# A new order for the first slots of a cross attention, and f32 products as three bf16 products in a local attention

## The chip, the cores and the metric

The kernel runs on one core of a Trainium2 chip. The metric is the device time of one execution in microseconds, the median of several. The span of a profiled execution is a little shorter than its device time. One record of a trace says which engine did what from when to when: TensorE (PE, its weight loads PEld), VectorE (DVE), ScalarE (ACT), GpSimd (POOL) and SyncE (SP), whose queue here issues nearly all transfers.

## The reference, cut to what matters

The model has two layers on a state `x` of 4 batches x 128 tokens x 512. Layer 0: cross attention from the state (the latents) to 2048 context rows per batch, self attention, mixture of experts. Layer 1: a second cross attention, a local attention, a quantised feed-forward network. The change touches the first stage and the last but one.

```
# layer 0, cross attention (16 heads of 64); ctx: 4 x 2048 x 512
xn  = layernorm(ctx) * g_x + b_x
ln  = layernorm(layernorm(x)) * g_l + b_l         # the state is normed twice
q   = rmsnorm(ln @ Wq) ;  k, v = concat(xn @ Wkv, ln @ Wkv) ; k = rmsnorm(k)
x   = x + softmax(q k^T + mask) v @ Wout + bout
# layer 1, local attention
h   = layernorm(x)
q, k, v = h @ Wq.T + bq, h @ Wk.T + bk, h @ Wv.T + bv
ph  = running mean of h inside chunks of 32 tokens
pk, pv  = ph @ Wpk.T + bpk, ph @ Wpv.T + bpv
x   = x + attention over 16 best earlier tokens, the last one and the last phrase
```

## The kernel before

The kernel is written instruction by instruction with semaphores; each engine has its own instruction list, and the stages (`cross0_attend`, `self0`, `experts`, `cross1_attend`, `local1`, `ffn1`) follow one another with a barrier between them.

`cross0_attend` is a software pipeline over slots n. A slot of unit u (4 heads of one batch, 17 tiles of 128 rows, 16 units) is `project(n)` on TensorE: keys and values of one tile of 128 context rows (the 17th tile is the latents), in 12 products of bf16 pairs (high x high, high x low, low x high). ScalarE copies the result (`copies`), VectorE takes the low half of the values (`values_low`). Everything else is hung into the slots by tables: `ln_stat`, `ln_rstd`, `ln_norm`, `ln_turn` for the norm and transposition of one quarter (512 rows, j = 0 to 3) of a batch's context; `k_sum`, `k_norm`, `k_turn` for the norm and transposition of the keys; `k_max` for the row maxima; `q_unit`, `q_copy`, `q_norm`, `q_turn`, `q_store` for the queries, which are computed once for all batches; `w_part` for splitting the weights of four heads into high and low halves (`weights_high` on ScalarE, `weights_low` on GpSimd). Scores of tile n run 25 slots behind (`LAG`), so slots 0 to 24 have no scores; the maximum of a unit must be done (`less_maximum`) before slot 25. Slots -8 to -1 (`FIRST` on) are the head: they only bring the first context quarters and the latents.

The order inside a slot is that of each engine's list. On TensorE: `project`, `turn` of keys, `context` turns, `turn_latents`, `query_turn`, `query_product`, then values, scores, maxima. Key turns and context turns share one bank of PSUM (`KT` = 5), each waits until the one before it has been read (`before_turn`, `before_ln`). On VectorE: `values_low`, `key_low`, `maximum`, `key_norm`, `key_sum`, `context_norm`, `context_stat`, the latents' norm, the query steps. A step of SP's list waits like any other: what stands behind it is issued later.

The state is normed twice by the helper `Norm`: statistics, variance plus 1e-5, square root on ScalarE, reciprocal, scaling in place; in slots -7 and -6, that is on VectorE ahead of the scaling of context's first quarter. `turn_latents` and the latents' affine step (`latents_turned`) stand in slot -2, the first query product in slot 0.

In `local1` the state is normed (`Norm`), turned by the helper `Turn` (16 transpositions, ScalarE copies them to `HT` in f32), TensorE makes the prefix sums (`L2672`), then three projections of 4 outputs x 4 chunks in f32 (line 2685: q, k from `HT`, pk from `PT_`), scores, and two sets of values (line 2703). Four of the five weights are loaded during `cross1_attend`, the fifth at the stage's start. GpSimd has no part in it.

Of the kernel before, what the change touches and what calls it, by code (L numbers as in the profile page):

```python
# [15 lines left out]
P = 128  # L16
B = 4
# [99 lines left out]
def cross0_attend(nc, t, X, keep, sb, sem):  # L117
# [47 lines left out]
    junk = late_part(16, 1)  # L165
    Dg = late_part(17, 1).rearrange("p (h q) -> p h q", q=P)
    less = late_part(18, 1)
    ao = late_part(19, 2).bitcast(F32).rearrange("p (k n) -> p k n", n=256)

    q_sq = late_part(0, 4).bitcast(F32).rearrange("p (k n) -> p k n", n=512)  # L170
# [20 lines left out]
    ln = Norm(sb, sem, "a0ln")  # L191
# [50 lines left out]
    for u in range(UNITS):  # L242
        for j in range(5):
# [14 lines left out]
    for k in range(B * QN):  # L258
        q_unit[k].append(k)
        q_copy[k + 1].append(k)  # L260
    for b in range(B):
        q_norm[2 * b + 3].append(b)
        q_turn[2 * b + 4].append(b)
        q_store[2 * b + 5].append(b)
    for g in range(1, QUADS):
        w_part[2 * g - 2].append(g)
# [3 lines left out]
    for b in range(B):  # L270
        for j in range(4):
            at = 4 * j - 6 if b == 0 else NT0 * (4 * (b - 1) + j)
            delayed = b == 1 and j == 0
            for i in range(4):
# [3 lines left out]
                ln_turn[at + 1 + i if b == 0 else at + ((25, 26, 29, 30) if delayed else (16, 17, 21, 22))[i]]\  # L278
                    .append((b, j, i))
            ln_rstd[at if b == 0 else at + (17 if delayed else 9)].append((b, j))  # L280
            if b == 0:
                mask_block[10 + j].append((b, j))
# [52 lines left out]
    with nc.Block() as block:  # L335

        @block.sync
        def _(sp):
# [117 lines left out]
            sp.dma_start(L, t["x"].rearrange("b p d -> p b d")).then_inc(lx_in, 16)  # L456
# [3 lines left out]
            sp.dma_start(mcol8[:], t["mask0_col"]).then_inc(vec_in, 16)  # L460
# [8 lines left out]
            load(0, 2)  # L469
            weights(2)  # L470
            latents_out()
            latents(0)
            weights(3)
            load(0, 3)
            sp.wait_ge(zero_done, 2)
            for n in range(LAST):
                for b in q_store[n]:
                    queries_out(b)
                if n == 6:
                    queries(0)  # L480
                    queries(1)
                if n == 9:
# [8 lines left out]
                for b in range(1, B):  # L491
# [4 lines left out]
                    for j in range(4):  # L496
                        if n == ((7, 11, 32, 41)[j] if b == 1 else NT0 * (4 * (b - 1) + j) - 10):
# [16 lines left out]
        def _(pool):  # L514
# [39 lines left out]
            def weights_low(g):  # L554
                pool.wait_ge(w_hi_done, g + 1)
# [2494 lines left out]
```

## Time and profile before

| | |
|---|---|
| median of 3 runs | 2519.19 us (2517.22 to 2527.97) |
| the profiled execution | 2523.05 us, its span 2521.2 us |
| mean granted clock of TensorE | 0.963 |
| TensorE busy | 2302.3 us, 91% of the span |
| VectorE, ScalarE, GpSimd busy | 1821.0, 1566.5, 1129.7 us |
| first product of `project` | 37.68 us after the span's start |
| first `less_maximum` | 157.55 us |
| `local1`, from its first instruction to the last sum | 2357.3 to 2456.5 us |

The page cuts the span into 40 slices of 63 us; a digit is the busy share of a slice in tenths. Views of a stretch give the busy time of each engine in it. A timeline line has its start, its duration (of a group of instructions with "xN"), the engine, the line, what is written and read, and in brackets how long the engine had been idle and what ended that.

### The profile page before, as it was taken

Reading aid. Unit: us, or ns where it says so; the run is one execution under the profiler, and the core shown is the slowest. Engines: PE = TensorE matmul, PEld = TensorE weight load, DVE = VectorE, ACT = ScalarE, POOL = GpSimd, SP = SyncE. Lnnn points to the kernel's source line nnn. Section 1 sums busy time; section 2 is a strip of 40 time slices with the busy share of each in tenths; the row PEclk is TensorE's granted clock in tenths of the full one; section 3 lists DMA queues with packets and bytes.
Section 4 is the critical chain, followed back from the end, with each engine's and each line's share of the span. In section 5 each row is a group of like instructions: output and inputs, shape, how many; then the busy total and the mean of one; then the engine's idle time right before and its main releaser. Section 6 shows DMA issues by size and latency. Waiting matters only on the chain. (4 is left out here: it accounts for less than half of the span.)

```text
span 2521.2 us, 57561 instructions
## 1 busy us (share of the span) xinstructions
PE 2302.3 (91%) x21955; PEld 1492.9 (59%) x21955; DVE 1821.0 (72%) x3374; ACT 1566.5 (62%) x2925; POOL 1129.7 (45%) x897
## 2 busy tenths in 40 slices
PE   5899999999999999998888799994899899998795
PEld 2456656666566656665445677772567676776442
DVE  6778878887788777776363899986677777766236
ACT  4556666666666666665233599983477676787313
POOL 4546676667666664555000000004467676756100
PEclk9999999999999999999889799997999999998897
DMA  6323432233322321124330799975433444224002
GB/s 206 96 54 97 119 95 67 66 87 102 90 75 76 99 75 42 39 59 149 122 126 10 265 369 363 363 273 184 146 108 118 128 121 130 89 90 160 29 1 86
DMA packets 248819, 313.56 MB, mean 124 GB/s; under 512 B 63313, under 2 KB 174545, under 8 KB 247649
## 3 DMA queue, kind: packets, MB, share of 16 engines
q1 hardware_dynamic: 244592, 301.75, 37.0%
q10 hardware_dynamic: 3312, 6.03, 0.6%
q8 instruction: 175, 2.87, 0.5%
q0 software_dynamic: 640, 2.10, 0.3%
q14 instruction: 100, 0.81, 0.1%
HBM read 226.23 MB, written 47.91 MB: 109 GB/s over the span
## 5 line engine op out<-in xcount | busy, mean ns | idle before, releaser
L581 POOL TENSOR_TENSOR a_late<-a_late 128x512 bf16<-128x512 f32 x272 | 316.0, 1162 | 357.1 <-ACT a_late L641 356.4
L959 PE MATMUL ps<-w,a_xlo 128*128 128x512 bf16 x1088 | 412.4, 379 | 0.0
L957 PE MATMUL ps<-w,a_xhi 128*128 128x512 bf16 x1088 | 412.3, 379 | 0.0
L958 PE MATMUL ps<-w,a_xhi 128*128 128x512 bf16 x1088 | 412.3, 379 | 0.0
L2155 POOL TENSOR_TENSOR a_plo<-a_p,a_phi 128x512 bf16<-128x512 f32 x256 | 306.6, 1198 | 178.2 <-ACT a_phi L2192 169.4
L607 ACT ACTIVATE a_kraw<-ps 128x256 f32<-128x256 f32 x272 | 104.2, 383 | 367.9 <-PE ps L959 366.2
L2287 DVE CUSTOM_DVE_ANT_0 a_junk<-ps,a_biasrow 128x512 bf16<-128x512 f32 x256 | 175.9, 687 | 116.5 <-PE ps L2427 113.0
L718 DVE TENSOR_TENSOR a_v<-ps,a_v 128x256 bf16<-128x256 f32 x272 | 114.2, 420 | 160.9 <-ACT a_v L609 159.4
L2187 ACT ACTIVATE a_p<-ps,a_mcol 128x512 f32<-128x512 f32 x256 | 174.8, 683 | 86.8 <-PE ps L2445 78.9
L531 POOL TENSOR_TENSOR a_rn<-a_rn,a_power 128x16 f32<-128x16 f32 (+1 forms) x80 | 204.9, 2561 | 6.6
L732 DVE SCALAR_TENSOR_TENSOR a_kraw<-a_kraw,a_rn 128x1024 f32<-128x1024 f32 (+1 forms) x80 | 154.2, 1928 | 74.2 <-POOL a_rn L531 74.2
L637 ACT ACTIVATE a_late<-ps,a_mcol 128x512 f32<-128x512 f32 x256 | 178.8, 698 | 20.9 <-PE ps L1011 10.6
L784 DVE CAST ps<-a_late 128x512 f32<-128x512 bf16 x256 | 174.3, 682 | 12.2 <-ACT a_late L637 12.2
L959 PEld LDWEIGHTS ps<-w,a_xlo 128*128 128x128 bf16 x1088 | 106.5, 98 | 128.4
L958 PEld LDWEIGHTS ps<-w,a_xhi 128*128 128x128 bf16 x1088 | 106.4, 98 | 125.5 <-issue 2.7
L2410 PE MATMUL ps<-a_whi,c_hi 128*128 128x128 bf16 x1024 | 179.1, 220 | 1.3
L2410 PE MATMUL ps<-a_wlo,c_hi 128*128 128x128 bf16 x1024 | 178.8, 220 | 0.0
L2410 PE MATMUL ps<-a_whi,a_clo 128*128 128x128 bf16 x1024 | 178.7, 219 | 0.0
L641 ACT ACTIVATE a_late<-a_late 128x512 bf16<-128x512 f32 x272 | 171.3, 630 | 8.7
L760 DVE CUSTOM_DVE_ANT_0 a_late<-ps,a_mrow 128x512 bf16<-128x512 f32 x256 | 173.7, 679 | 0.7
L2192 ACT ACTIVATE a_phi<-a_p 128x512 bf16<-128x512 f32 x256 | 161.3, 630 | 8.1
L957 PEld LDWEIGHTS ps<-w,a_xhi 128*128 128x128 bf16 x1088 | 106.5, 98 | 99.3 <-issue 1.7
(444 smaller groups left out, 6882.7 us busy)
## 6 DMA issues: line engine op xcount, KB each, us to landing
e_wst<-in_L_ffn_W SPq DMA_DIRECT2D x46, 2048.0 KB, 10.4
a_ks<-a_khi SPq DMA_DIRECT2D x256, 64.0 KB, 2.0
a_ks<-a_klo SPq DMA_DIRECT2D x256, 64.0 KB, 2.0
a_ct<-in_ctxT SPq DMA_DIRECT2D x16, 1024.0 KB, 7.3
a_ks<-k1h_d SPq DMA_DIRECT2D x128, 128.0 KB, 2.5
xa<-in_ctx SPq DMA_DIRECT2D x8, 1024.0 KB, 5.7
a_xn<-in_ctx SPq DMA_DIRECT2D x8, 1024.0 KB, 5.5
k1h_d<-a_khi SPq DMA_DIRECT2D x64, 128.0 KB, 1.9
```

What stands on the lines that cost most here:

```text
L531: pool.tensor_tensor(rn[:, key_part(j)], rn[:, key_part(j)], power[:, key_part(j)], ALU.pow)\
L581: pool.tensor_tensor(p_lo[:, m % 3, :], p32[:, m % 2, :], p_hi[:, m % 3, :], ALU.subtract)\
L637: act.activation(p32[:, m % 2, :], ps[:, m % 2, :], ACT.Exp, **bias).then_inc(exp_done, 1)
L760: dve.tensor_tensor_reduce(junk[:], ps[:, bank_m(x), :], mrow[:, j * 512:(j + 1) * 512], 1.0, -3e38, ALU.add, ALU.max, mx[:, h, j:j + 1]). ...
L784: dve.tensor_copy(ps[:, m % 2, :], less[:]).then_inc(seeded, 1)
L957: pe.matmul(out, x_hi[:, c, tile], w_hi[:, c, g, :], start=(c == 0), stop=False)
L958: pe.matmul(out, x_hi[:, c, tile], w_lo[:, c, g, :], start=False, stop=False)
L959: last = pe.matmul(out, x_lo[:, c, tile], w_hi[:, c, g, :], start=False, stop=(c == C - 1))
L2155: pool.tensor_tensor(p_lo[:, m % 3, :], p32[:, m % 2, :], p_hi[:, m % 3, :], ALU.subtract)\
L2187: act.activation(p32[:, m % 2, :], ps[:, m % 2, :], ACT.Exp, bias=mcol[:, u // 4, s:s + 1])\
L2287: dve.tensor_tensor_reduce(junk[:], ps[:, bank_m(x), :], biasrow[:, u // 4 % 2, j * 512:(j + 1) * 512], 1.0, -3e38, ALU.add, ALU.max, mx[: ...
L2410: last = pe.matmul(ps[:, VP, i * P:(i + 1) * P], x[:, b % 2, c, tile], w[:, 1, c, quad], start=(c == 0 and k == 0), stop=(c == C - 1 and k ...
```

## The change

Two parts. In `cross0_attend`:

- The two norms of the latents become one with its own variance: norm of a norm has the variance v/(v+e), and `1.0 + 1e-5` and `1e-10` account for both (`latents_stat`, `latents_norm`). Their place is behind context's first quarter.
- The low half of the first weight is made by VectorE, behind context's first quarter; those of weights 1 to 3 are made in slots 3, 6, 9 (before 0, 2, 4) by GpSimd.
- The second quarter's turns go to slots 0, 1, 2, 2 (before -1 to 2), `turn_latents` to slot 1, all query steps two slots later, the first key turns to slots 10 to 13 (before 8 to 11), the maxima of quarters 0 to 2 two per slot from slot 14 (before those of quarters 0 and 1, from slot 12).
- In the slot, context turns that follow key turns go behind the query product, and the second context turn of a slot too.
- SP's list: first weight ahead of the state, second quarter ahead of it too, third quarter ahead of the small loads of the query norms.

In `local1`: tokens, prefix means and the five weights are each split into a high and a low half in bf16, and each f32 product becomes three bf16 products. ScalarE makes high halves, VectorE the tokens' low halves, GpSimd the rest.

```diff
-                    k_turn[e + (5 if (u, j) == (0, 0) else 3) + pr].append((u, j, pr))
+                    k_turn[e + ((7, 5, 3, 3)[j] if u == 0 else 3) + pr].append((u, j, pr))
                 for h in range(4):
-                    k_max[12 + 2 * j + h // 2 if u == 0 and j < 2 else e + 5 + h].append((u, j, h))
+                    k_max[14 + 2 * j + h // 2 if u == 0 and j < 3 else e + 5 + h].append((u, j, h))
...
-        q_unit[k].append(k)
-        q_copy[k + 1].append(k)
+        q_unit[k + 2].append(k)
+        q_copy[k + 3].append(k)
...
-        w_part[2 * g - 2].append(g)
+        w_part[3 * g].append(g)
...
-            at = 4 * j - 6 if b == 0 else NT0 * (4 * (b - 1) + j)
+            at = (-6, -3, 2, 6)[j] if b == 0 else NT0 * (4 * (b - 1) + j)
...
-                ln_turn[at + 1 + i if b == 0 else at + ((25, 26, 29, 30) if delayed else (16, 17, 21, 22))[i]]\
+                ln_turn[at + ((3, 4, 5, 5)[i] if j == 1 else 1 + i) if b == 0 else at + ((25, 26, 29, 30) if delayed else (16, 17, 21, 22))[i]]\
...
             load(0, 0)
-            sp.dma_start(L, t["x"].rearrange("b p d -> p b d")).then_inc(lx_in, 16)
             weights(0)
...
             load(0, 1)
+            sp.dma_start(L, t["x"].rearrange("b p d -> p b d")).then_inc(lx_in, 16)
...
             weights(1)
+            load(0, 2)
             for dst, src in ((gq, t["L0_xattn_qn_g"]), (gk, t["L0_xattn_kn_g"])):
...
             latents_out()
+            load(0, 3)
             latents(0)
             weights(3)
-            load(0, 3)
...
                 if n == -6:
-                    ln.vector(dve, step, L, L, 2)
+                    dve.wait_ge(w_hi_done, 1)
+                    dve.tensor_tensor(w_lo[:, :, 0, :], wst[:, 0], w_hi[:, :, 0, :], ALU.subtract).then_inc(w_lo_done, 1)
+                if n == -4:
+                    latents_stat()
                 if n == -2:
+                    latents_norm()
+                if n == 1:
                     latents_low()
...
+                ahead = 0 if k_turn[n] else 1
+                for b, j, c in ln_turn[n][:ahead]:
+                    context(b, j, c)
                 for k in q_unit[n]:
                     query_product(k)
+                for b, j, c in ln_turn[n][ahead:]:
+                    context(b, j, c)
```

and in `local1`:

```diff
+            def weights_low(k):
+                pool.wait_ge(w_hi_done, k + 1)
+                pool.tensor_tensor(w_lo[:, k], w[k], w_hi[:, k], ALU.subtract).then_inc(w_lo_done, 1)
+
+            weights_low(0)
+            weights_low(1)
+            for c in range(C):
+                pool.wait_ge(pt_hi_done, c + 1)
+                pool.tensor_tensor(pt_lo[:, c, :], PT_[:, c, :], pt_hi[:, c, :], ALU.subtract).then_inc(pt_lo_done, 1)
+            for k in range(2, 5):
+                weights_low(k)
...
+            weights_high(0)
             norm.scalar(act)
-            turn.scalar(act, ps, HT)
+            for c in range(C):
+                act.wait_ge(h_turn, c + 1)
+                act.activation(ht_hi[:, c, :], ps[:, c, :], ACT.Copy).then_inc(ht_hi_done, 1)
+            weights_high(1)
...
             norm.vector(dve, step, Hn, X)
+            for c in range(C):
+                dve.wait_ge(ht_hi_done, c + 1)
+                dve.tensor_tensor(ht_lo[:, c, :], ps[:, c, :], ht_hi[:, c, :], ALU.subtract).then_inc(ht_lo_done, 1)
...
                 for c in range(C):
-                    last = pe.matmul(ps[:, 4 + n % 2, :], w[k][:, c, o * P:(o + 1) * P],
-                                     (HT if k < 2 else PT_)[:, c, :], start=(c == 0), stop=(c == C - 1))
+                    pe.matmul(out, w_hi[:, k, c, cols], hi[:, c, :], start=(c == 0), stop=False)
+                    pe.matmul(out, w_hi[:, k, c, cols], lo[:, c, :], start=False, stop=False)
+                    last = pe.matmul(out, w_lo[:, k, c, cols], hi[:, c, :], start=False, stop=(c == C - 1))
...
                 for c in range(C):
-                    last = pe.matmul(ps[:, bank_v(n), :], (HT, PT_)[k][:, c, b * P:(b + 1) * P], w[3 + k][:, c, :],
-                                     start=(c == 0), stop=(c == C - 1))
+                    pe.matmul(out, hi[:, c, tok], w_hi[:, 3 + k, c, :], start=(c == 0), stop=False)
+                    pe.matmul(out, hi[:, c, tok], w_lo[:, 3 + k, c, :], start=False, stop=False)
+                    last = pe.matmul(out, lo[:, c, tok], w_hi[:, 3 + k, c, :], start=False, stop=(c == C - 1))
```

ScalarE makes the high half of a prefix chunk ahead of each of the first four evacuations, and those of weights 2 to 4 ahead of the fifth, seventh and ninth.

## Rows read from the trace of the kernel before

**Rows 1.** The page, the granted clock of TensorE in 40 slices.

```profile
PEclk9999999999999999999889799997999999998897
```

**Rows 2.** TensorE's waits in the first 200 us: total, times, longest.

```profile
PE ps L976 <- DVE xa L749: 23.2, 1, 23.2
PE ps L976 <- DVE a_klo L738: 6.4, 3, 2.5
PE ps L976 <- ACT a_xf L625: 4.8, 3, 2.9
PE ps L976 <- DVE a_xn L749: 1.8, 1, 1.8
```

**Rows 3.** Timeline of TensorE in the head: start, duration, instruction.

```profile
29.23 1.09 PE L976 MATMUL ps<-identf,xa 128*128 128x128 f32 x4 [0.96 <-ACT a_xf L625]
...
31.28 1.09 PE L976 MATMUL ps<-identf,xa 128*128 128x128 f32 x4 [0.96 <-ACT a_xf L625]
...
32.16 3.20 PE L1052 MATMUL ps<-identf,a_ks 128*128 128x128 f32 x16
...
37.68 0.38 PE L957 MATMUL ps<-w,a_xhi 128*128 128x512 bf16 x1
...
40.05 0.38 PE L959 MATMUL ps<-w,a_xlo 128*128 128x512 bf16 x1
```

**Rows 4.** Timeline of the other engines in the head.

```profile
12.11 2.44 DVE L81 BATCH_NORM_STATS2 a0ln_stats<-a_ks 128x6 f32<-128x512 f32 x4
...
12.63 1.06 POOL L540 TENSOR_TENSOR a_rstd<-a_rstd,a_power 128x4 f32<-128x4 f32 x1
...
15.31 1.89 ACT L645 ACTIVATE w<-a_v 128x2048 bf16<-128x2048 f32 x1
...
15.65 1.92 DVE L90 TENSOR_SCALAR a_ks<-a_ks,a0ln_mv,a0ln_rstd 128x512 f32<-128x512 f32 x4
17.29 4.19 POOL L556 TENSOR_TENSOR w<-a_v,w 128x2048 bf16<-128x2048 f32 x1 [3.59 <-ACT w L645]
17.60 5.53 DVE L749 TENSOR_SCALAR xa<-xa,a_mv,a_rstd 128x512 f32<-128x512 f32 x4
...
33.75 2.77 ACT L651 ACTIVATE a_ks<-ps,a_bl,a_gl 128x512 f32<-128x512 f32 x4
34.32 1.16 POOL L547 TENSOR_TENSOR a_xlo<-a_xf,a_xhi 128x512 bf16<-128x512 f32 x1
...
37.21 2.50 DVE L817 TENSOR_TENSOR a_late<-a_ks,a_late 128x512 bf16<-128x512 f32 x4
```

**Rows 5.** Transfers issued from 4.3 to 6.1 us: KB each, us to landing.

```profile
a_v<-in_L_xattn_Wkv SPq DMA_DIRECT2D x2, 512.0 KB, 9.4
```

**Rows 6.** Timeline of TensorE, slots 1 to 24: a query product, one collision, the first maximum.

```profile
47.17 3.60 PE L1063 MATMUL ps<-a_ks 128*128 128x512 f32 x8
...
103.68 0.63 PE L976 MATMUL ps<-identf,a_xn 128*128 128x128 f32 x4 [2.51 <-DVE a_klo L738]
...
157.55 0.39 PE L1022 MATMUL ps<-a_late,onesb 128*128 128x512 bf16 x1 [1.48 <-DVE a_late L770]
```

**Rows 7.** Local attention by stretches: length, busy time of PE, PEld, DVE, ACT, POOL, clock.

```profile
2357.25:2370.01 12.76, 7.16 (x48) 7.00 (x49) 7.18 (x17) 3.88 (x6) 0.00 (x0) 0.65 0.43 144
2370.01:2412.16 42.15, 41.37 (x99) 18.06 (x97) 0.83 (x3) 8.28 (x13) 0.00 (x0) 1.00 0.00 0
...
2419.40:2446.87 27.47, 27.47 (x66) 12.12 (x65) 16.15 (x46) 2.02 (x8) 0.00 (x0) 1.00 0.00 1
```

**Rows 8.** Timeline of local attention, ScalarE and VectorE.

```profile
2357.27 1.28 ACT L95 ACT_TABLE_LOAD   x1 [8.41 <-PEq L2931]
...
2360.88 1.91 DVE L90 TENSOR_SCALAR l_h<-xa,ln_mv,ln_rstd 128x512 f32<-128x512 f32 x4
...
2438.07 0.68 DVE L2655 TENSOR_TENSOR l_wt<-l_shift,l_z 128x512 f32<-128x512 f32 x1
```

**Rows 9.** Timeline of TensorE, the first product of slot 4.

```profile
63.53 0.38 PE L957 MATMUL ps<-w,a_xhi 128*128 128x512 bf16 x1
```

More of the change, by code:

```diff
@@ L164, in cross0_attend @@
     p_lo = late_part(13, 3).rearrange("p (k n) -> p k n", n=512)
[L165 to L168, printed above, removed]
+    Dg = late_part(16, 1).rearrange("p (h q) -> p h q", q=P)
+    less = late_part(17, 1)
+    ao = late_part(18, 2).bitcast(F32).rearrange("p (k n) -> p k n", n=256)
+    junk = late_part(20, 1)
     q_sq = late_part(0, 4).bitcast(F32).rearrange("p (k n) -> p k n", n=512)
@@ L693, in _ @@
                 if n == -2:
+                    act.wait_ge(l_var_ready, 1)
+                    act.activation(l_rstd[:], l_var[:], ACT.Sqrt).then_inc(l_sd_ready, 1)
+                if n == 1:
                     latents_turned()
@@ L812, in add_result, with latents_stat, latents_norm @@
                 dve.tensor_tensor(X[:, b, :], X[:, b, :], ps[:, bank_o(b), :], ALU.add).then_inc(res_done, 1)
+            def latents_stat():
+                dve.wait_ge(lx_in, 16)
+                for b in range(B):
+                    last = dve.bn_stats(l_st[:, b, :], L[:, b, :])
+                step(last)
+                for b in range(B):
+                    last = dve.bn_aggr(l_mv[:, b, :], l_st[:, b, :])
+                step(last)
+                dve.tensor_scalar(l_var[:], l_mv[:, :, 1], 1.0 + 1e-5, 1e-10, ALU.mult, ALU.add).then_inc(l_var_ready, 1)
+            def latents_norm():
+                dve.wait_ge(l_sd_ready, 1)
+                step(dve.reciprocal(l_rstd[:], l_rstd[:]))
+                for b in range(B):
+                    dve.tensor_scalar(L[:, b, :], L[:, b, :], l_mv[:, b, 0:1], l_rstd[:, b:b + 1],
+                                      ALU.subtract, ALU.mult).then_inc(l_normed, 1)
             def latents_low():
@@ L1048, in turn_latents @@
             def turn_latents():
-                pe.wait_ge(ln.done, 2 * B)
+                pe.wait_ge(l_normed, B)
                 for c in range(C):
@@ L1082, in _ @@
                     turn(u, j, pr)
-                for b, j, c in ln_turn[n]:
-                    context(b, j, c)
-                if n == -2:
+                if n == 1:
                     turn_latents()
@@ L2537, in local1 @@
     Hn = sb("l_h", [P, B, D], F32)
-    HT = sb("l_ht", [P, C, TOK], F32)
+    ht_hi = sb("l_hthi", [P, C, TOK], BF16)
+    ht_lo = sb("l_htlo", [P, C, TOK], BF16)
     PT_ = sb("l_pht", [P, C, TOK], F32)
+    pt_hi = sb("l_pthi", [P, C, TOK], BF16)
+    pt_lo = sb("l_ptlo", [P, C, TOK], BF16)
+    w_hi = sb("l_whi", [P, 5, C, D], BF16)
+    w_lo = sb("l_wlo", [P, 5, C, D], BF16)
     w4 = sb("l_w4", [P, C, D], F32)
-    w = [keep["lw"][:, k] for k in range(4)] + [w4]
+    w = [keep["lw"][:, k] for k in range(4)] + [w4[:]]
     bc = sb("l_bc", [P, 3, C], F32)
@@ L2561, in local1 @@
     norm = Norm(sb, sem, "ln")
-    turn = Turn(sem, "lt", C, [0, 1, 2, 3])
+    h_turn, ht_hi_done, ht_lo_done = sem("l_hturn"), sem("l_hthi_d"), sem("l_htlo_d")
+    pt_hi_done, pt_lo_done = sem("l_pthi_d"), sem("l_ptlo_d")
+    w_hi_done, w_lo_done = sem("l_whi_d"), sem("l_wlo_d")
     w_in = keep["lw_in"] + [sem("l_w_in4")]
@@ L2665, in _ @@
             pe.wait_ge(norm.done, B)
-            turn.tensor(pe, ps, Hn, identf)
+            for c in range(C):
+                for b in range(B):
+                    last = pe.transpose(ps[:, c, b * P:(b + 1) * P], Hn[:, b, c * P:(c + 1) * P], identf[:])
+                last.then_inc(h_turn, 1)
             pe.wait_ge(c_in, 7 * 16)
@@ L2674, in _ @@
                 last.then_inc(pf_mm, 1)
-            pe.wait_ge(turn.copied, C)
+            pe.wait_ge(ht_lo_done, C)
             for n in range(3 * C):
```

65 lines of the change are left out of this document (39 added, 26 removed).

## The prediction

> **What bounds the kernel now.** The times come first, then the page by slices, then TensorE's waits in the stretch that the change touches, then that stretch in order of time, then the same for local attention. The slices [rows 1] show TensorE at full clock through the first quarter, and the page has it busy for most of every slice there: moving the end of the head means removing TensorE idle time or TensorE work, and nothing else. The waits of the first 200 us [rows 2] name all of the idle time: 23.2 us before the first transposition, 4.8 us between transpositions of context's first quarter, 1.8 us before the second quarter, 6.4 us in three waits where context's transposition follows a key transposition into the same bank, and 1.5 us at the first maximum [rows 6]. Smaller ones are 0.15, 0.35 and 0.83 us. From the first product at 37.7 us [rows 3] to slot 24 the engine otherwise runs without a hole, and after 158 us no wait of any length is left. So whatever the head gains by slot 24 is carried to the end.
>
> Local attention is read by stretches [rows 7]: TensorE is busy for 41.4 of 42.15 us in the three projections and for all 27.47 us of the values, and GpSimd does nothing at all. Here the work on TensorE itself is the bound.
>
> **Local attention.** The 48 and 32 products in f32 appear as 96 and 64 records: 27.47 us for 64 of them is 0.429 us a record, 0.858 us a product [rows 7]. A bf16 product of the same 512 columns, with a weight load ahead of each, starts every (40.05-37.68)/11 = 0.2155 us [rows 3], so three are 0.646 us. Projections: 48 x 0.212 = 10.2 us saved; values: 32 x 0.212 = 6.8 us; together 17.0 us.
>
> What it adds goes to other engines. ScalarE's cast of a 2048-column weight takes 1.89 us and GpSimd's low half 4.08 to 4.19 us [rows 4]. Weights 1 to 4 are needed at 10-us steps or later (a projection of one weight is now 16 x 0.646 = 10.3 us), so their casts (one every two outputs of 2.6 us, beside a 0.7-us evacuation) and low halves are hidden; without that cover a late low half would cost up to its 4.1 us, once. The prefix's low halves (four of 1.16 us on GpSimd) are wanted only at output 8, 20 us later. The low halves of the tokens are on VectorE, 0.68 us each, one behind each ScalarE copy; the last ends about 0.7 us after the old last copy, and the prefix's own division queues behind it, while TensorE does the prefix products. I charge 0.3 us.
>
> The first weight's low half is not free. It starts when ScalarE's cast ends, about 2359.2 (or 1.3 us later if the table load comes first), and lasts 4.1 us, that is over the norm's four scalings, which now start at 2360.88 and take 1.91 us [rows 8]. The head shows what such a pair does: with GpSimd's low half at 17.29 to 21.48, four identical scalings took 5.53 us instead of 1.92 [rows 4]: they ended 1.65 us behind GpSimd's end. Applied here, the scalings end at 2363.3 + 1.7 = 2365.0 or, table load first, 2366.3, against 2362.79: +2.2 to +3.5 us. If the variance's small operation is caught as well, it is +3.2 us. I take 2.9 us. (The Trainium skill, "SBUF — State Buffer", section "Who interferes with whom", says that VectorE in a two-port mode and GpSimd lock each other out for a whole instruction; the trace agrees by the 5.53 us. By a rule of no interference the sum would be 2.9 us better.)
>
> The tail starts behind the values still: the softmax chain's last step ended at 2438.75 [rows 8], 8.1 us before the values' end at 2446.87, and had itself waited for values; with values 6.8 us shorter at least 1.3 us are left. Local attention: -17.0 + 2.9 + 0.3 = **-13.8 us**.
>
> **The head, up to the first product.** Removed from VectorE ahead of context's norm: the first latent norm (2.44 + 0.4 + 0.2 + 1.92 us) [rows 4]. GpSimd's inverse root for quarter 0 was ready at 13.69, but the scalings began at 17.60 and ran into GpSimd's low half. Now they start at 13.75 and end at 15.7; GpSimd has no weight's low half then. The first weight's low half moves to VectorE behind them: by the 512-column rows (2.50 us for four) about 2.4 us, ready at 18; its weight lands sooner, as it goes from third to second in the queue (it took 9.4 us from issue as third [rows 5], and the transfer ahead of it, of the same size, is gone), and its cast is done well before 15.7. Four contexts turned at the pitch 31.28-29.23 = 2.05 us start at 15.75; the 3.3 us hole of the latents' Sqrt on ScalarE, which stood in the second one, is gone. Start of the last 21.9, its high half ends 2.6 us later, its low half on GpSimd (1.16 us) at 25.7. GpSimd's inverse root of quarter 1 is ahead of it in the queue but is done by 23. First product at **25.8 us against 37.7**.
>
> **The head, the first slots.** TensorE had done 3.2 us of latent transpositions and 0.6 us of context before the old first product [rows 3]; these come after it now. The 16 latent transpositions took 3.20 us, 0.2 us each; at full rate a record of a quarter of the columns of the f32 ones takes 0.429/4 = 0.107 us. So that stretch was at half rate; now the first product group pays this (4.3 us, not 2.6), and the latents take 1.8. Slot 0: product 25.8 to 30.1, context 30.6. Slot 1: product 33.2, latents 35.0, context 35.5. ScalarE then copies the slot, evacuates one context and only then the latents: 2.77 us for their affine step, ending at 39.8 [rows 4]. Slot 2: product 38.1, context 38.6, then the first query product waits 1.2 us for it, and ends at 43.3 (3.45 us, [rows 6]); the next context waits 0.6 us, because ScalarE first makes the latents' four high halves. Slot 3: 44.5 to 51.1. Before, slot 3 ended at 63.53 [rows 9], with two more query products (6.9 us) done. 63.5 - (51.1 + 6.9) = 5.5 us gained. Both ends: 7.3 us without the two waits; 3 us if quarter 1's norm, which shares VectorE with the latents' statistics (3.0 us) and GpSimd's low halves, is 2.5 us later than my 27.0.
>
> SP's queue: quarter 2 is now issued when quarter 0 has been turned (23 us, before 32.4), ahead of the four tiny query-norm loads, whose issue took 6.5 us; the latents' stores and their wait end near 50, and quarter 3 lands at 55.5, where slot 4's statistics begin: level, at worst 1 us. All loads of weights 1 to 3 have 20 us or more of slack.
>
> **The head, slots 4 to 24.** Key turns move from slots 8 to 11 to slots 10 to 13 while context's stay at 7 to 10, so three collisions (6.4 us, the 2.51 us row among them [rows 6]) become one, at slot 10, and there the query turn of 0.9 us now stands between: about 1.6 us stay. The maxima of quarter 2 now come two a slot: VectorE needs about 3.8 us in such a slot and TensorE 3.5, so another 0.3 us. The waits at the end (0.83 and 1.48 us) are VectorE's own chain and stay. Before 9.2 us of waits from slot 4 on, after 4.6: 4.6 us gained; bounds 2 us (two collisions left) and 6.4 us. Query products, turns and stores keep their work and move by two slots with everything that waits for them. Head: -5.5 - 4.6 = **-10.1 us**, bounds -5 and -13.7.
>
> **Sum.** The profiled execution took 2523.05 us around a span of 2521.2; -10.1 - 13.8 = -23.9 gives a span of 2497.3 and 2499.2 for that execution. It stands 3.9 us above the median of the runs, and from the median 2519.19 the same sum gives **2495.3 us**.
>
> **Rivals.** (A) The head returns nothing: the slots are paced by a chain that the new order lengthens (queries two slots later, maxima doubled), and the 5.5 us flow back before slot 24. Against it speaks that TensorE was idle for only 9.2 of the 94 us there. 2519.2 - 13.8 = 2505.4, 10%. (B) Local attention gains less, since a low half is late each time: one missed 4.1-us low half and one collision more; 2495.3 + 6 = 2501, 13%. (C) The head does better, no wait of the latents and no collision left: 2495.3 - 3.6 - 1.6 = 2490, 12%. (D) Slower: TensorE's clock. The stretch at 2357 us has a granted clock of 0.65, and full-rate stretches follow it [rows 7]; after an idle time of 7.7 us its 16 transpositions run at 1.2 GHz. If the wait for the low halves of the tokens, short as it is, sent the clock back and it stayed at 1.2 GHz, the 51.7 us of bf16 products would take 103: from 0.46 of them at the low level on the whole change is lost, from 0.71 on it is slower by more than 0.5%, and with all it is 2547. Against: waits of 2.5 us in the head left the clock at 1.00. 3%. (The Trainium skill, "TensorE: Matmul & The Clock Gate", "HAM oscillation — how this bites in real kernels", describes a clock that falls at every wait for data; no row here has it.) My sum holds 62%.
>
> **Numbers.** The likeliest case alone is 2490 to 2500. Eight in ten needs A's upper part and C: 2488 to 2505. What a measurement of this kernel can tell from no change is about 0.5%, 12.6 us, a bound at 2506.6. A lies at it, half of its spread on either side: faster 0.93, same 0.05, slower 0.02.
>
> **What would show it.** First product near 25.8 us; first query product waiting about a microsecond for ScalarE's latents; the first maximum (now at 157.55) near 147.5; one wait of context for a key's low half instead of three. In local attention: the four scalings delayed or stretched to 4 or 5 us beside GpSimd's first low half, 144 and 96 bf16 products at 0.2155 us, and no wait at the weights' low halves. The prediction is wrong if the first maximum comes later than 153, if the head's products start after 30 us, or if the bf16 products show another pitch.

## The result, and the profile of the changed kernel

The changed kernel takes 2503.73 us, the median of 5 runs (2501.19 to 2509.05), against 2519.19 us of 5 runs of the kernel before (2517.22 to 2527.97). The ratio is 0.9927, with a 95% interval of 0.9911 to 0.9944: 18.4 us less by the ratio, 15.5 us by the medians, where 23.9 us were forecast. Its profiled execution took 2503.7 us around a span of 2501.8 us.

The local attention gave nearly what was forecast. The head gave its first part and then lost it again. TensorE's waits of the first 200 us in the changed kernel (for what, us in all, times, longest), the answer to [rows 2]:

```profile
PE ps L1000 <- DVE xa L754: 15.8, 1, 15.8
PE ps L1098 <- DVE a_late L856: 6.9, 3, 3.5
PE ps L981 <- POOL a_xlo L552: 3.1, 1, 3.1
PE ps L1000 <- ACT a_xf L629: 2.9, 3, 1.0
PE ps L1046 <- DVE a_late L775: 1.5, 1, 1.5
PE ps L1087 <- ACT a_ks L655: 1.2, 1, 1.2
PE ps L1015 <- DVE a_mx L765: 1.1, 2, 0.7
PE ps L1019 <- DVE a_mx L765: 0.8, 1, 0.8
```

The first wait is 15.8 us where it was 23.2 us. The three waits of context's transposition for a key's low half (6.4 us in [rows 2]) are gone altogether. In their place stands a line that the kernel before did not have: 6.9 us in three waits of the query turn (L1098) for VectorE's scaling of the queries (L856). Those places in TensorE's timeline of the changed kernel, to be held against [rows 3, 6, 9]:

```profile
26.29 0.58 PE L981 MATMUL ps<-w,a_xhi 128*128 128x512 bf16 x1 [3.15 <-POOL a_xlo L552]
...
39.82 3.70 PE L1087 MATMUL ps<-a_ks 128*128 128x512 f32 x8 [1.18 <-ACT a_ks L655]
...
50.76 0.38 PE L982 MATMUL ps<-w,a_xhi 128*128 128x512 bf16 x1
...
67.89 1.09 PE L1098 MATMUL ps<-identf,a_late 128*128 128x128 f32 x8 [1.66 <-DVE a_late L856]
...
99.68 1.09 PE L1098 MATMUL ps<-identf,a_late 128*128 128x128 f32 x8 [3.55 <-DVE a_late L856]
...
110.74 1.09 PE L1098 MATMUL ps<-identf,a_late 128*128 128x128 f32 x8 [1.67 <-DVE a_late L856]
...
154.30 0.39 PE L1046 MATMUL ps<-a_late,onesb 128*128 128x512 bf16 x1 [1.48 <-DVE a_late L775]
```

The first product starts at 26.29 us (forecast 25.8) and the first query product waits 1.18 us (forecast 1.2). The record of slot 4's first product is missing; the second starts at 50.76, so slot 4 begins 0.22 us earlier, at 50.54 us; with the two query products not yet done, 6.9 us, that is 57.4 against 63.53 [rows 9]: 6.1 us gained so far. The first maximum comes at 154.30 instead of 157.55 [rows 6]: only 3.25 us are left of it. Why is seen on VectorE in slots 9 and 10 of the changed kernel:

```profile
90.25 0.42 DVE L723 TENSOR_TENSOR a_v<-ps,a_v 128x256 bf16<-128x256 f32 x1 [1.77 <-ACT a_v L613]
94.04 0.69 DVE L748 BATCH_NORM_STATS2 a_st<-xa 128x6 f32<-128x512 f32 x1 [3.37 <-DMA xa<-in_ctx]
94.77 0.18 DVE L749 BATCH_NORM_AGGREGATE a_mv<-a_st 128x2 f32<-128x6 f32 x1
94.87 0.65 DVE L844 TENSOR_REDUCE a_ks<-a_late 128x8 f32<-128x512 f32 x1
95.44 0.24 DVE L854 RECIPROCAL a_ks<-a_ks 128x16 f32<-128x16 f32 x1
95.71 3.92 DVE L856 TENSOR_TENSOR a_late<-a_late,a_ks 128x1024 f32<-128x1024 f32 x1
99.55 0.41 DVE L723 TENSOR_TENSOR a_v<-ps,a_v 128x256 bf16<-128x256 f32 x1
99.89 0.68 DVE L743 TENSOR_TENSOR a_klo<-ps,a_khi 128x512 bf16<-128x512 f32 x1
```

and on GpSimd, the low half of the fourth group's weights:

```profile
94.49 4.06 POOL L562 TENSOR_TENSOR w<-a_v,w 128x2048 bf16<-128x2048 f32 x1 [1.72 <-ACT w L649]
```

VectorE runs its slot in the order in which it is written. The statistics of the next batch's first quarter (L748) stand ahead of the query scaling, and here they wait 3.37 us for their transfer, which in the new order is issued in the slot that reads it. Beside the edits described above, the load of that quarter moved from slot 7 to slot 9 of SyncE's list, while its statistics kept slots 9 and 10. SyncE in the changed kernel, then SyncE and VectorE in the kernel before, where 16.7 us lay between the two:

```profile
88.60 0.44 SPq L348 DMA_DIRECT2D xa<-in_ctx  x1
```

```profile
86.73 0.44 SPq L343 DMA_DIRECT2D xa<-in_ctx  x1
...
103.45 0.68 DVE L743 BATCH_NORM_STATS2 a_st<-xa 128x6 f32<-128x512 f32 x1
```

So in the changed kernel the scaling starts at 95.71, behind the start of GpSimd's low half, and lasts 3.92 us where it takes 1.22 to 1.23 us elsewhere (109.46 us, for one): it could not finish before GpSimd's instruction ended at 98.55, and did so 1.1 us later. TensorE stands for 3.55 us, and its granted clock falls. The changed kernel's stretches (length, busy time of PE, PEld, DVE, ACT, POOL, granted clock):

```profile
63.50:99.60 36.10, 30.82 (x126) 15.55 (x127) 22.62 (x37) 20.79 (x41) 18.76 (x10) 1.00 0.23 73
99.60:105.40 5.80, 5.72 (x24) 3.21 (x25) 2.26 (x6) 3.53 (x6) 1.94 (x3) 0.71 0.09 23
105.40:154.30 48.90, 43.39 (x218) 21.97 (x222) 40.74 (x93) 19.28 (x55) 21.76 (x14) 1.00 0.35 95
```

In the 5.8 us behind the wait the granted clock is 0.71 of 2.4 GHz, so a part of them ran at 1.2 GHz, which costs 5.8 x 0.29 = 1.7 us of work (an estimate).

Local attention of the changed kernel, its first and the next stage's first instruction and the norm, against [rows 8] (timelines of ScalarE, VectorE and GpSimd):

```profile
2350.76 1.91 ACT L2637 ACTIVATE l_whi<-c_hi 128x2048 bf16<-128x2048 f32 x1 [8.43 <-PEq L3004]
...
2352.75 4.05 POOL L2623 TENSOR_TENSOR l_wlo<-c_hi,l_whi 128x2048 bf16<-128x2048 f32 x1 [9.19 <-ACT l_whi L2637]
...
2353.70 3.13 DVE L86 TENSOR_SCALAR ln_var<-ln_mv 128x4 f32<-128x4 f32 x1
2357.10 0.18 DVE L88 RECIPROCAL ln_rstd<-ln_sd 128x4 f32<-128x4 f32 x1 [0.27 <-ACT ln_sd L95]
2357.32 1.91 DVE L90 TENSOR_SCALAR l_h<-xa,ln_mv,ln_rstd 128x512 f32<-128x512 f32 x4
...
2437.78 1.28 ACT L2873 ACT_TABLE_LOAD   x1 [9.00 <-PEq L3004]
```

and by stretches, against [rows 7]: up to the first product, the projections, the values.

```profile
2350.76:2367.28 16.52, 7.94 (x48) 7.71 (x50) 12.93 (x22) 8.10 (x9) 5.87 (x2) 0.61 0.33 112
2367.28:2399.75 32.47, 31.59 (x147) 14.52 (x149) 2.35 (x2) 15.89 (x19) 19.06 (x8) 1.00 0.00 1
2406.50:2427.00 20.50, 20.40 (x94) 9.32 (x95) 15.97 (x46) 2.02 (x8) 0.00 (x0) 1.00 0.00 0
```

The stage lasts 2437.78 - 2350.76 = 87.02 us. Before, it lasted from 2357.27 to 2457.54, 100.27 us: 13.25 us gained, of 13.8 forecast. The bounds of the three stretches are not quite those of [rows 7]. The scores start at 2399.09 us, so the second stretch holds 0.66 us of them; and the record of the first product of both groups is missing, which puts their starts at 2367.07 and 2406.33; the values end at 2427.05. With the bounds of [rows 7] the projections shrank from 42.15 to 32.0 us and the values from 27.47 to 20.7, and the way to the first product grew from 12.8 to 16.3 us: 10.1 + 6.75 - 3.55 = 13.3 us.

### The profile page after: what moved, and what is told of

Same layout as the page of the kernel before. It is cut to its first block and busy times, and to the rows that moved or that the text cites. A ratio compares the mean times of both kernels' runs of the same rounds, so it can differ in the third digit from the quotient of the medians.

```text
span 2501.8 us, 57450 instructions
## 1 busy us (share of the span) xinstructions
PE 2273.9 (91%) x21752; PEld 1489.4 (60%) x22035; DVE 1821.4 (73%) x3365; ACT 1579.5 (63%) x2934; POOL 1150.1 (46%) x905
```

## The experiments

Beside each time stands the kernel before on the same chip in the same session: 2524.52 us (17 runs) for the first four kernels, 2522.60 us (8 runs) for the second four, 2523.98 us (11 runs) for the last four.

**Which part gave what.** Two kernels: the kernel before with the new local attention alone, and the changed kernel with the old one.

> The kernel before with the new local attention alone. Theory (the parts add, and local attention gave what the profile shows, 100.25 to 87.0 us from its first instruction to the next stage's): the stage takes 87.0 us again, the first maximum stays at 157.5 us, and the time falls by 13.3 us, a ratio of 0.9947. Rival (the 4.5 us by which the second cross attention was shorter in the profile of the changed kernel belongs to the change, by way of loads or of the stage's length): the ratio is 0.993 or less and that stage, from 1730.1 to 2357.3 us before, is shorter here too.

> The changed kernel with the old local attention. Theory (the head gave 3.3 us by slot 24 and 1.6 at the end of its stage): first product at 26.3 us, first maximum at 154.3 us, self attention starts at 1213.6 us against 1215.2, local attention takes 100.3 us, and the ratio is 0.9993, not to be told from no change. Rival (the head's gain is larger and the profiled execution hid it): self attention starts at or before 1211 us and the ratio is 0.998 or less.

Local attention alone: 2510.85 us, ratio 0.9951 (0.9938 to 0.9964), the stage 87.42 us long. The head alone: 2521.55 us, 0.9990 (0.9979 to 1.0001), its first maximum at 154.35 us. So what can be measured is the local attention; the head's 11 us at the first product are worth about 2.5 us at the end, with an interval that includes nothing at all. Of the rival's two signs for the first kernel one is there: the second cross attention took 622.8 us against 627.1. But that length goes either way in later kernels (627.7 us in one with the new local attention, 623.0 in one with the old), and the other sign, a ratio of 0.993 or less, is missing. The same kernel has the head of the kernel before, and so gives a second execution of it: its first maximum comes at 160.38 us, not at 157.55. Its granted clock from 90 to 115 us, and then that of the kernel before in the same stretch:

```profile
90.00:115.00 25.00, 18.64 (x91) 10.46 (x90) 13.95 (x23) 13.85 (x31) 11.09 (x7) 0.93 0.34 100
```

```profile
90.00:115.00 25.00, 18.64 (x103) 10.74 (x102) 14.48 (x25) 14.36 (x33) 13.41 (x8) 1.00 0.31 92
```

The same collisions (1.96, 2.51 and 1.90 us) let the clock fall in one execution and not in the other. Of the 2.83 us between the two, 1.24 were there when slot 4 began (64.77 us against 63.53); the other 1.6 came behind that, and the clock accounts for them (25 x 0.07 = 1.75 us, an estimate). The head of the kernel before therefore reaches its first maximum at 157.6 or 160.4 us, and what a new head gains has to be read against both.

**Is it the late statistics?** The statistics of the next batch's first quarter two slots later.

```diff
-ln_stat[... at + ((9, 10, 13, 13) if delayed else ...
+ln_stat[... at + ((11, 12, 13, 13) if delayed else ...
```

> The changed kernel, with the statistics of the next batch's first quarter two slots later (slots 11 and 12 in place of 9 and 10), so that VectorE doesn't wait in slot 9 for a transfer issued in slot 9. Theory (that wait of 3.37 us made the query's scaling late, and its being late put it behind GpSimd's low half of a weight, where it took 3.92 us in place of 1.22): VectorE's wait and the stretching are both gone, the query turn of slot 10 waits for nothing or below 0.5 us instead of 3.55, context behind it waits about 1.5 us for the key's low half, and the first maximum is at 152 us against 154.3. Rival (the lock alone holds the turn; the low half comes when it comes): the scaling is still stretched and the first maximum stays within 0.5 us of 154.3.

The wait for the transfer went, the scaling of slot 9 started at 94.01 and took 1.22 us, and the turn of slot 10 waited for nothing. But the first maximum stayed at 154.76 us: context now waited 1.02 us for a key's low half in that slot, a key turn 0.80 us behind it, and the statistics, moved to slot 11, stood ahead of the next scaling there. Counted from the start of slot 4, which came 1.07 us later in this execution, 0.6 us were gained. TensorE in slot 12 of this kernel:

```profile
109.53 1.80 PE L1098 MATMUL ps<-identf,a_late 128*128 128x128 f32 x8 [2.75 <-DVE a_late L856]
```

2.75 us where it had been 1.67, and the clock fell behind this wait instead (0.76 from 108 to 115 us). The cause of the one wait was right; taking it away there only handed it on. The ratio, 0.9919 (0.9905 to 0.9933), can't be told from the changed kernel's 0.9927.

**Is it the scaling's place?** Three edits of the changed kernel, one each: the scaling ahead of the statistics on VectorE; the query turn last on TensorE; GpSimd's low halves in other slots.

```diff
 # VectorE, each slot
+for b in q_norm[n]:
+    query_norm(b)
 for b, j, i in ln_stat[n]:
     context_stat(b, j, i)
 ...
-for b in q_norm[n]:
-    query_norm(b)
```

> The changed kernel with VectorE's scaling of the queries put ahead of the statistics of the contexts in a slot's order (slots 5, 7, 9 and 11). Theory (the waits of the key/context collisions were handed to the query turns, because the scaling stands last in VectorE's slot): the turn of slot 6 waits 0 instead of 1.66 us, the scaling of slot 9 starts near 94.0 and takes 1.22 instead of 3.92, the turn of slot 10 waits nothing, with 1.0 left at the context behind it as where the statistics came later; the turn of slot 12 keeps its 1.67, since no statistics stand in slot 11. Waits from slot 4 on 6 us instead of 10.3, first maximum near 150.5 instead of 154.3, time 4 us under the changed kernel (ratio to the kernel before 0.991). Rival (the first maximum is held by something later than these waits, as the run with the later statistics hints): the waits fall, the first maximum stays within 1 us of 154.3 and the time within 1 us.

```diff
 # TensorE, each slot
-for b in q_turn[n]:
-    query_turn(b)
 ...
 (contexts)
+for b in q_turn[n]:
+    query_turn(b)
```

> The changed kernel with TensorE's query turn put behind the contexts' transposes in slots 4 to 12. Theory: what stands ahead on VectorE decides, not TensorE's order: the turn of slot 6 loses its 1.66, but in slot 10 the key's low half stands behind the same scaling of 3.92 us, so the context waits about 4 us for that low half where the turn waited 3.55; slot 12's 1.67 stays. First maximum 153 to 154. Rival (TensorE's order alone costs these waits): slot 10 waits under 1 us and the first maximum comes near 150.

```diff
 for g in range(1, QUADS):
-    w_part[3 * g].append(g)
+    w_part[2 * g + 2].append(g)
```

> The changed kernel with GpSimd's low halves of the second to fourth group in slots 4, 6 and 8 instead of 3, 6 and 9. Theory (the scaling of slot 9 is held by GpSimd's instruction in the same slot, the late statistics only push it there): with no low half in slot 9 the scaling takes 1.22 instead of 3.92, and the turn of slot 10 waits 3.55 - 2.70 = 0.85. First maximum 1.5 to 2.7 us before 154.3. Rival (the transfer holds the scaling, the lock is by the way): the scaling takes 1.22 but the turn waits over 2 us. A low half in slot 8 may stretch slot 9's key scaling instead.

With the scaling first, VectorE in slot 9 (timeline) and the stretch from 90 to 115 us:

```profile
92.73 1.23 DVE L856 TENSOR_TENSOR a_late<-a_late,a_ks 128x1024 f32<-128x1024 f32 x1
93.87 0.69 DVE L748 BATCH_NORM_STATS2 a_st<-xa 128x6 f32<-128x512 f32 x1
```

```profile
90.00:115.00 25.00, 21.23 (x110) 11.62 (x109) 16.55 (x29) 15.71 (x36) 16.02 (x9) 1.00 0.40 120
```

The turns of slots 6 and 10 wait for nothing, context 1.02 us and a key turn 0.79 us in their place, the clock stays at 1.00, and the first maximum comes at 151.00 us: 3.3 us earlier. It would be more, had this execution not been 1.3 us later when slot 4 began (51.84 us against 50.54), by a longer stretch at half rate behind the first product. From there to the first maximum it takes 99.16 us instead of 103.76, 4.6 us less: the waits are 7.3 us instead of 10.3, and the clock gives the other 1.7. The time is 2498.10 us, ratio 0.9907 (0.9890 to 0.9923), which by itself can't be told from the changed kernel's. The rows show the place where the head lost its gain. The turn of slot 12 waits 1.95 us, a little more than before.

With the turn last on TensorE the wait did not go, it changed its name, as the theory had it:

```profile
100.48 1.08 PE L1000 MATMUL ps<-identf,a_xn 128*128 128x128 f32 x4 [4.58 <-DVE a_klo L743]
```

4.58 us instead of 3.55; first maximum 154.63, just above the 153 to 154 expected, one run of 2509.99 us. TensorE's order is not what counts here.

With the low halves in slots 4, 6 and 8 the scaling of slot 9 took 1.23 us beside a wait of 3.14 us for the transfer, and the turn of slot 10 waited 0.63 us. The turn's wait is 2.9 us shorter, and 2.7 us of that are the scaling's own duration (3.92 - 1.23), as expected: this is the share of GpSimd's instruction. Yet the first maximum came at 153.91, 0.4 us earlier instead of 1.5 to 2.7. Of the miss, 1.2 us lie before slot 4, which began at 51.73 us; from there on 1.6 us were gained. More did not come because the clock from 90 to 115 us was 0.86. It fell behind the turn of slot 12, which had waited 1.95 us, and it did not fall behind the same wait in the kernel with the scaling first. That place in this kernel, then in the other:

```profile
107.48 1.97 PE L1098 MATMUL ps<-identf,a_late 128*128 128x128 f32 x8 [1.95 <-DVE a_late L856]
```

```profile
107.44 1.09 PE L1098 MATMUL ps<-identf,a_late 128*128 128x128 f32 x8 [1.95 <-DVE a_late L856]
```

One run: 2506.19 us.

**Is the low half on VectorE worth anything?** GpSimd makes the first low half again, at the place in the order where the kernel before had it.

```diff
 # GpSimd, context_low's slots
+if n == FIRST + 2:
+    weights_low(0)
 # VectorE
-if n == -6:
-    dve.wait_ge(w_hi_done, 1)
-    dve.tensor_tensor(w_lo[:, :, 0, :], wst[:, 0], w_hi[:, :, 0, :], ALU.subtract)...
```

> The changed kernel with the low half of the first group's weights put back from VectorE to GpSimd, at the place in the order where the kernel before had it. Theory (the head's first slots gain because VectorE is not locked by that instruction): GpSimd holds it for about 4.1 us from 14.0 on, the first context scalings stretch to about 4 us instead of 1.92 each pair of reads, the first product comes 2 to 4 us later than 26.3, and the time is 1 to 3 us over the changed kernel. Rival (statistics, root and transfers alone set the first product): first product within 0.5 us of 26.3, since VectorE gets 2.3 us free instead.

VectorE and GpSimd in this kernel:

```profile
14.11 5.65 DVE L756 TENSOR_SCALAR xa<-xa,a_mv,a_rstd 128x512 f32<-128x512 f32 x4 [1.55 <-POOL a_rstd L545]
```

```profile
14.32 4.25 POOL L562 TENSOR_TENSOR w<-a_v,w 128x2048 bf16<-128x2048 f32 x1 [0.25 <-ACT w L651]
```

The four scalings take 5.65 instead of 1.92 us, the first product starts at 30.09, 3.8 us later, and the first maximum at 159.70 us. The time is 2511.91 us, ratio 0.9955 (0.9941 to 0.9970), as with the local attention alone (0.9951). Without this one move the rearrangement of the head is worth nothing that these runs could measure. Outside the expectation, which gave 1 to 3 us over the changed kernel: by the two ratios it is 7 us (0.9955 against 0.9927), more than the landmarks account for, and the loss grew from 3.8 us at the first product to 5.4 us at the first maximum, with a clock of 0.86 from 90 to 115 us.

**The lock in local attention.** GpSimd's first low half waits for VectorE's norm.

```diff
+pool.wait_ge(norm.done, B)
 weights_low(0)
```

> The changed kernel, with GpSimd's first low half in local attention held until the norm's scalings are done. Theory (GpSimd's instruction held VectorE's small variance operation for 3.13 us in place of 0.17): that operation takes 0.17 us, the stage takes 84.0 us against 87.0, and no product waits for the low half. Rival (the low half is then late for the first projection, since it starts at the scalings' end and takes 4.1 us): the first projection waits, and the stage stays above 86 us.

VectorE and GpSimd in this kernel:

```profile
2348.18 0.17 DVE L86 TENSOR_SCALAR ln_var<-ln_mv 128x4 f32<-128x4 f32 x1
2348.91 1.91 DVE L90 TENSOR_SCALAR l_h<-xa,ln_mv,ln_rstd 128x512 f32<-128x512 f32 x4
```

```profile
2350.90 4.08 POOL L2623 TENSOR_TENSOR l_wlo<-c_hi,l_whi 128x2048 bf16<-128x2048 f32 x1 [12.85 <-DVE l_h L90]
```

The variance's step is back from 3.13 to 0.17 us, no product waits for the later low half, and the stage takes 83.76 us: 3.26 us less. The ratio of 0.9917 (0.9902 to 0.9932) agrees with that, but its interval does not prove it by itself; the rows do.

**Together.** The two edits that gained, in one kernel; to it the scaling ahead of the keys' sum too; or GpSimd's low halves by slots; and the mended head with the old local attention.

> The two edits that gained, together: VectorE's scaling of the queries ahead of the statistics, and in the local attention GpSimd's first low half of the weights behind VectorE's norm. Theory (both act on waits in different stages, so they add): first maximum near 151.0, local attention 83.8 us from its first instruction to the next stage's, and a ratio to the kernel before of 0.990, some 3.3 + 3.3 = 6.6 us under the changed kernel by the stages' own times. Rival (one of them only shifts a wait into the stages between): ratio stays at 0.9907 or above.

> As the run before it, and the scaling of the queries also ahead of the sum of the keys' squares (1.21 us) in VectorE's order. Theory (the turn of slot 12 waits 1.95 us because that sum stands ahead of the scaling in slot 11): that wait falls to about 0.7 us and the first maximum comes near 150.0. Rival (ScalarE's root, last in its own order, sets the scaling's start): the wait falls by less than 0.3 us, since the scaling waits for the root wherever it stands, and now the sum of the keys waits behind it; first maximum 151 or later.

> As the first of these three, with GpSimd's low halves in slots 4, 6 and 8. Theory (with the scaling ahead, no low half holds it any more in either order): no change of the waits of slots 6 and 10, first maximum within 0.5 us of 151.0 and the time within 1 us. Rival (the low half in slot 8 now holds the next slot's work): first maximum 1 us or more later.

> The head's part of the change alone, with the old local attention, and the scaling of the queries ahead of the statistics. The head alone gave 0.9990 of the kernel before. Theory: with the query turns' waits gone the head is worth what its first slots promised, first maximum near 151.0 against 154.35, so 3.3 us more: ratio 0.9977. Rival (the earlier first maximum is given back in the steady state by the pitch of the later slots): ratio within 0.0005 of 0.9990.

All the runs, by landmarks of their profiled executions (us) and by their timed ratio:

| kernel | first product | slot 4 | clock, 90 to 115 | first maximum | local attention | ratio (95%) |
|---|---|---|---|---|---|---|
| before | 37.68 | 63.53 | 1.00 | 157.55 | 100.27 | 1 |
| changed | 26.29 | 50.54 | 0.93 | 154.30 | 87.02 | 0.9927 (0.9911-0.9944) |
| local attention alone | 37.99 | 64.77 | 0.93 | 160.38 | 87.42 | 0.9951 (0.9938-0.9964) |
| head alone | 26.36 | 50.54 | 0.93 | 154.35 | 100.52 | 0.9990 (0.9979-1.0001) |
| statistics later | 26.30 | 51.61 | 0.93 | 154.76 | 87.34 | 0.9919 (0.9905-0.9933) |
| low half after norm | 26.34 | 50.82 | 0.93 | 154.36 | 83.76 | 0.9917 (0.9902-0.9932) |
| scaling first | 26.60 | 51.84 | 1.00 | 151.00 | 86.93 | 0.9907 (0.9890-0.9923) |
| turn last on TensorE | 26.64 | 52.19 | 0.93 | 154.63 | 87.01 | one run |
| low halves by slots | 26.32 | 51.73 | 0.86 | 153.91 | 86.80 | one run |
| low half on GpSimd | 30.09 | 55.18 | 0.86 | 159.70 | 86.81 | 0.9955 (0.9941-0.9970) |
| scaling first, low half after norm | 26.43 | 51.20 | 1.00 | 150.38 | 84.57 | 0.9907 (0.9894-0.9921) |
| and before the keys' sum | 26.62 | 52.19 | 1.00 | 151.35 | 83.93 | 0.9906 (0.9891-0.9920) |
| instead, low halves by slots | 26.29 | 50.46 | 1.00 | 149.25 | 84.35 | 0.9891 (0.9874-0.9908) |
| head alone, scaling first | 26.39 | 51.08 | 1.00 | 150.25 | 100.66 | 0.9955 (0.9942-0.9968) |

The column "slot 4" is the start of its first product; where that record is missing, 0.22 us before the second. With the head of the kernel before, two more query products (6.9 us) are done by then. From slot 4 to the first maximum it takes 102.2 to 104.5 us in the seven kernels with the new head and the scaling in its old place, and 98.8 to 99.2 us in the five with the scaling first. What the first maxima differ by beyond that lies before slot 4, in the stretch at half rate behind the first product, which was 2.9 us long in the changed kernel (26.29 to 29.16 us) and over 4 us in others.

The landmarks add up nearly as expected (150.38 us for 151.0, 84.57 for 83.8), the ratio did not fall below 0.9907. Putting the scaling ahead of the keys' sum too was worth nothing: the turn of slot 12 waits 0.70 instead of 1.96 us, as expected, but a key turn now waits 1.37 us for VectorE. From slot 4 to the first maximum it is 99.16 us against 99.18; the first maximum 1 us later, the rival's sign, was already there at slot 4. The low halves by slots brought the first maximum 1.1 us forward, more than the 0.5 expected, but 0.7 us of it before slot 4. This is the fastest kernel, 2495.19 us (2492.66 to 2504.42): under the kernel before, and with its interval just under the changed kernel's (0.9908 against 0.9911), though that one was measured in another session. The mended head alone gave 0.9955, 11.6 us, where 0.9977 was expected; its first maximum, 7.3 or 10.1 us ahead of the two seen with the old head, explains most of that, and the expectation had been worked out from 0.9990, which has an interval of its own of 2.8 us either side.

## Why the forecast went as it did

**The total** of 2495.3 us was 8.4 us too low. The measured 2503.73 us lie inside the range given, 2488 to 2505, but only in the part that rival A was to cover (2505.4, 1.7 us away); the likeliest case's own range, 2490 to 2500, missed them. And the prediction's own sign of being wrong, a first maximum later than 153 us, is there: 154.30. The direction and the range held, the mechanism in the head did not.

**Local attention, -13.8: right, at -13.25.** Projections 42.15 - 32.0 = 10.1 us (10.2 forecast), values 6.75 (6.8). The norm ended 8.47 us after the stage's start instead of 5.52, +2.95 for a forecast of 2.9. That the sizes agree so well is partly luck: the forecast took them from four stretched scalings, but what GpSimd's instruction caught was the variance's step on four numbers, which the text had named beside its sum, and the scalings kept their 1.91 us. TensorE's first product came another 0.6 us later than that, where 0.3 us were charged, mostly because VectorE's division of the prefix sums stands behind the tokens' low halves. No weight's low half was waited for. The rule of the Trainium skill cited for this term ("SBUF — State Buffer", "Who interferes with whom") is that the two engines lock each other out for a whole instruction; the trace agrees, with 3.13 us for 0.17 here, and 5.65 for 1.92 in the kernel with the low half on GpSimd.

**The head to slot 4, -5.5: right, at -6.1.** First product, the half-rate stretch behind it and the wait for the latents came within 0.5 us. In the other kernels with these first slots, slot 4 began up to 1.65 us later, so that the same sum gives 4.4 to 6.2 us; the agreement to a few tenths is that of one execution.

**The head, slots 4 to 24, -4.6: wrong, this is the step that failed.** Instead of 4.6 us gained, 6.1 - 3.25 = 2.9 us were lost against the kernel before's profiled execution. The waits there are 10.3 us, against 9.2 before and 4.6 forecast. The sentence that failed is "Query products, turns and stores keep their work and move by two slots with everything that waits for them": the query scaling did not move with everything. It moved into slots where VectorE had statistics ahead of it that wait for a transfer, and where GpSimd makes a weight's low half. The collision of key and context at slot 10 was counted, and the query turn taken as a filler of 0.9 us in it; it was the one that waited, 3.55 us. The experiment with the scaling first shows this cause: it alone brings the first maximum forward by 3.3 us, and shortens these slots by 4.6. With it they gain 94.02 + 6.9 - 99.16 = 1.8 us; the rest of the 4.6 forecast is waits, 7.3 us instead of 4.6, those of 1.02, 0.79 and 1.95 us among them. By the rows, the late transfer goes back to the load that moved to slot 9 without its statistics; that is not shown by an experiment, since no kernel with the load in slot 7 or 8 was run. Of the gap of 7.45 us between forecast and profile in these slots (4.6 + 2.85), the waits make 5.7 and the clock behind the long one 1.7.

**Rival A, that the head returns nothing,** was put at 10% and named the right place, "queries two slots later", but not the mechanism: what lengthened was VectorE's slot, not the chain of the maxima. For the head alone it is nearly what happened (0.9990), and for the sum too: 2519.19 - 13.25 - 3.25 = 2502.7 us, where 2503.73 were measured. The head of the kernel before was read from one execution; in the other execution the first maximum comes 2.8 us later, 1.6 us of that behind the start of slot 4, with the lower clock. Against that one the change gained 6.1 us by slot 24 and not 3.25.

**Rival D, the clock,** was dismissed with "waits of 2.5 us in the head left the clock at 1.00". That rested on a single execution. Eight profiled executions have a wait of 2.5 us or more between 90 and 115 us, and in seven of them the granted clock of that stretch was 0.86 or 0.93; the eighth is the one that was read. In the five with the scaling first, whose longest wait there is 1.37 to 1.96 us, it was 1.00. The wait's length alone does not decide it: behind 1.95 us the clock fell in one kernel and not in another. In local attention, where the rival had placed it, nothing of the kind happened.

**Whatever the head gains by slot 24 is carried to the end: right** as far as its own stage goes. From the first maximum to the next stage's first instruction it is 1057.7 us before (1215.21 - 157.55) and 1059.3 us after (1213.58 - 154.30), and between 1056.7 and 1059.7 us in the other twelve. The stages behind add a scatter that is not the change's: the second cross attention, the same code in all, took 627.1 us before, 622.6 after and 616 to 628 in the experiments. So the two spans differ by 19.4 us, more than the 16.5 us that head and local attention give; what is left belongs to that scatter.

**Open.** Why the clock was 0.86 with a longest wait of 1.95 us, in the kernel whose only edit is the low halves in slots 4, 6 and 8, how much of the 1.7 us by which the clock helps the kernels with the scaling first is the edit's and how much is chance, and what in the last session's timed runs keeps the two combined edits at 0.9907, when the landmarks are some 3 us better than with one of them, stays open; intervals of 3 to 4 us either side allow both.

## What to carry to other kernels

When work is moved by whole slots, write out each engine's new slot in order and ask of each instruction what now stands ahead of it: one that waits for a transfer holds up everything written behind it, and the wait shows under the name of whoever needed that. When a load moves, look where its readers stand. A wait that is taken away on the engine that shows it often reappears next door; move the late instruction ahead of the one that waits instead. And keep VectorE's short steps on a critical path away from a long GpSimd instruction: starting the latter when the former are done cost nothing and gave 3.3 us in one stage, and moving it to VectorE 3.8 us in the other.

## What the runs showed of the hardware that was not expected

A VectorE step on 128x4 numbers, 0.17 us alone, took 3.13 us because GpSimd's 4.05-us instruction had begun 0.95 us before it: the smallest instruction pays the whole rest. A two-input step from memory (the query scaling, 1.22 us) paid in the same way, 3.92 us, while a sum with one input (L844) just ahead of it, beside the same GpSimd instruction, kept its 0.65 us. And the granted clock of the same code with the same waits differed between two executions, 1.00 and 0.93 over 25 us: 1.75 us. Behind the same wait of 1.95 us the eight records of TensorE's next transpositions took 1.97 us in one kernel and 1.09 in another.
